# A six-layer decoder on one core: last norms moved into the neighbouring stages, and router logits by column groups

## The chip, the cores and the metric

The kernel runs on 1 core of one Trainium2 chip. The metric is the device time of one execution in microseconds (us), as the median of several runs. The engines are TensorE (PE in the profile; PEld is its weight load), VectorE (DVE), ScalarE (ACT), GpSimd (POOL) and SyncE (SP), which here only issues DMAs.

## The reference, cut to what matters

x is 16 x 128 x 256 (2048 rows of 256 channels). The last two of six sublayers and their norms are the ones that the change touches:

```python
    x = _layernorm(x + _L1_attn_ref(...), axis=-1)
    x = _layernorm(x + _L1_xattn_ref(x, ctx_2048, ...), axis=-1)   # n4 in the kernel before
    x = _layernorm(x + _L1_ffn_ref(x, w_gate, w1, w3, w2), axis=-1)  # n5 in the kernel before
    return x

    def _L1_ffn_ref(hidden_states, w_gate, w1, w3, w2):
        x = hidden_states.reshape(-1, H)                 # 2048 x 256
        logits = x @ w_gate                              # 256 x 8
        logits = SOFTCAP * jnp.tanh(logits / SOFTCAP)
        probs = jax.nn.softmax(logits, axis=-1)
        _, idx = jax.lax.top_k(probs, TOPK)              # 2 of 8 experts
        weights = probs * jax.nn.one_hot(idx, E).sum(-2)
        for e in range(E):
            h = jax.nn.silu(x @ w1[e]) * (x @ w3[e])
            out = out + h @ w2[e] * weights[:, e:e + 1]
```

_layernorm subtracts a row's mean and divides by the root of its variance plus 1e-5, with no gain and no offset.

## The kernel before, in words

The rows are held in SBUF as X[p, b, c]: 16 batches b of 128 rows, a row per partition p. The program is a chain of layers. Each is a block with one instruction stream per engine, written out by hand in program order, and semaphores between the streams. Between two layers `layer` frees the semaphores and all engines meet at a barrier (L139). The layers at the end are `quant_layer` (its main part is `attention`), `norm_layer` "n4", `moe_layer` and `norm_layer` "n5".

`attention` has 128 units: 8 head groups w by 16 batches b, u.n = 16 w + b. `in_steps` writes out, on each engine, steps 0, 1, 2, ...; in step s a stage with lag k works on unit s - k. On PE the stages of a step are queries(0), keys_values(0), turn_p(3), turn_q(1), output(5), turn_k(1), values(3), scores(1). queries writes the bank bQ (L1387, L1388) and may begin once DVE's apply_q (L1607) has read the unit before. output (L1464) needs z from POOL (L1582); DVE's residual (L1651) adds its result to X. In the last head group, w = 7, the row's value is final with the residual, and DVE takes its statistics (row_stats, L1655). After unit 127 has entered there are five more steps, in which fewer and fewer stages have work: the drain.

n4 (L203 and on) first works out from row_stats the means and deviations of 8 batches at a time on DVE (L371 to L376), takes the power -0.5 on POOL (L351), and scales the rows on DVE (L385, six of eight batches) and ACT (L328, two). SP loads the router's weights moe_gate and the first four pieces (1 MB each) of the experts' weights w1 and w3 (L1685, into w_low), and stores the normed rows to two DRAM tensors, sums and rows_x (L1697). PE runs three products that only keep it busy (L288), transposes X (L301), and multiplies it with the gate: 32 products with 128 rows of XT as the stationary operand and 8 moving columns (L280). Its groups of four batches wait for copies from PSUM by ACT (L322) and DVE (L395). The weights w1, w3 are split into high (rounded, fp32r) and low (what is left) halves, piece by piece: ACT makes high (`split_high`, L1703), DVE low (`split_low`, L1708), and for the four pieces in BY_PE PE makes low (`subtract`, L1810 and L1811) and ACT copies it back (`keep`, L1900).

`moe_layer` first works out the routing: DVE's chain L1969 to L2046 (softmax, top two, a place for each row in tiles of 128 rows of one expert), with counts and a map made on PE (L1818, L1825). Then POOL gathers the rows of a tile from rows_x (L1950), PE transposes them (L1850), multiplies by w1 and w3 (`up`, L1863 to L1865), transposes (L1873) and multiplies by w2 (`down`, L1884), and POOL adds the result to sums in DRAM (L1960), one add after the other (semaphore d_add). There are 39 tiles. Before the first tile PE waits for the routing, for all halves of the weights and for w2.

n5 loads sums back in two halves (L244), takes statistics (L366), scales, and stores the output in two halves (L249).

## Time and profile before

| | us |
|---|---|
| median of 3 runs (lowest, highest) | 1529.4 (1528.71, 1534.27) |
| the profiled execution | 1539.61 |
| its span, first to last instruction | 1537.8 |
| mean granted TensorE clock, of 2.4 GHz | 0.943 |
| PE busy in the span | 1375.2 (89%) |
| DVE busy | 1077.0 (70%) |
| ACT busy | 930.2 (60%) |
| POOL busy | 816.5 (53%) |

The page's shares are means over layers that have different limits; what counts here is which wait ends last at the places that are changed. The profiled execution is 10.2 us longer than the median of the timed ones. Of the program's 1537.8 us the attention ends at 1235.5, n4 runs from 1236.6 to 1261, the experts' layer from 1262.0 to about 1510, and n5 from 1514.5 to the end.

### The profile page before, as it was taken

To read this page: it belongs to the slowest core of one execution; us is meant where nothing else is said; L and a number is where in the kernel's file an instruction comes from. 1 tells how busy PE (TensorE), PEld (TensorE's weight loads), DVE (VectorE), ACT (ScalarE), POOL (GpSimd) and SP (SyncE) were. 2 spreads that over 40 slices of the span, in tenths; PEclk is the share of its full clock that TensorE was granted. 3 is DMA by queue.
4 is the path that set the end of the run, shared out by engine and by line. 5 is a ranking of instruction groups with operands and counts; after the bars stand their busy time and mean duration, and the time that the engine had idled before them with its cause. 6 is when DMAs were issued, how large, how long until landed. Compare 5 with 4: busy or idle time off the path is not lost. (4 is left out here: it accounts for less than half of the span.)

```text
span 1537.8 us, 27930 instructions
## 1 busy us (share of the span) xinstructions
PE 1375.2 (89%) x8307; PEld 1112.7 (72%) x8324; DVE 1077.0 (70%) x2565; ACT 930.2 (60%) x3122; POOL 816.5 (53%) x853
## 2 busy tenths in 40 slices
PE   7599467998579999999999999999999978999990
PEld 3343355765248999999988888888888765888880
DVE  1599676887577888888888887778888746333323
ACT  3199315776447878788887777777777735232220
POOL 2377103654206767677796676756765511455441
PEclk9699789999689999999999999999999969999996
DMA  3363001000010100001001010000000067333323
GB/s 124 115 227 132 31 26 42 2 1 1 1 42 1 43 1 29 26 1 46 12 24 51 1 42 1 29 14 1 1 1 1 1 213 245 48 50 52 52 42 117
DMA packets 45811, 72.76 MB, mean 47 GB/s; under 512 B 3772, under 2 KB 32388, under 8 KB 43364
## 3 DMA queue, kind: packets, MB, share of 16 engines
q1 hardware_dynamic: 32804, 44.00, 8.6%
q0 software_dynamic: 7488, 10.23, 4.2%
q10 hardware_dynamic: 5376, 16.78, 2.9%
q8 instruction: 71, 1.16, 0.3%
q14 instruction: 72, 0.59, 0.1%
HBM read 50.94 MB, written 20.05 MB: 46 GB/s over the span
## 5 line engine op out<-in xcount | busy, mean ns | idle before, releaser
L1513 ACT ACTIVATE pr_<-ps,neg_ 128x128 f32<-128x128 f32 x512 | 181.4, 366 | 68.4 <-DVE neg_ L1621 67.6
L1571 POOL TENSOR_TENSOR rstd<-var,half 128x6 f32<-128x6 f32 x128 | 172.2, 1345 | 10.2 <-POOL var L1566 0.4
L1530 ACT ACTIVATE y<-ps,invsm 128x128 bf16<-128x128 f32 x512 | 145.9, 369 | 24.7 <-PE ps L1453 24.5
L1582 POOL TENSOR_TENSOR z<-t,m 128x512 fp32r<-128x512 f32 x128 | 148.6, 1161 | 4.0 <-DVE t L1647 4.0
L1566 POOL TENSOR_TENSOR var<-stat,deps 128x6 f32<-128x6 f32 x128 | 25.5, 199 | 230.8 <-DVE stat L1601 230.8
L1435 PE MATMUL ps<-qkt 128*128 128x128 f32 x1024 | 145.4, 285 | 2.3 <-ACT qkt L1497 1.2
L1435 PEld LDWEIGHTS ps<-qkt 128*128 128x128 f32 x1024 | 124.8, 192 | 29.6 <-issue 26.9
L1464 PE MATMUL ps<-phi,z 128*128 128x256 f32 x512 | 138.9, 303 | 3.6 <-POOL z L1582 3.4
L1575 POOL TENSOR_TENSOR pr_<-pr_,rec_ 128x512 f32<-128x512 f32 x128 | 133.5, 1043 | 4.7 <-DVE rec_ L1628 4.7
L1453 PE MATMUL ps<-XT 128*128 128x256 f32 x512 | 132.1, 381 | 2.2 <-ACT XT L1521 2.2
L1464 PE MATMUL ps<-plo,z 128*128 128x256 f32 x512 | 128.3, 283 | 0.0
L1596 DVE BATCH_NORM_STATS2 stat<-ps 128x6 f32<-128x256 f32 x256 | 97.7, 424 | 33.9 <-PE ps L1388 33.8
L1621 DVE TENSOR_REDUCE neg_<-ps 128x4 f32<-128x512 f32 x128 | 88.5, 691 | 41.9 <-PE ps L1435 41.9
L1960 POOL DMA_INDIRECT sums<-f_ys,f_ids x39 | 61.8, 1583 | 105.0 <-PE ps L1850 83.3
L1387 PE MATMUL ps<-whi,xq 128*128 128x512 f32 x256 | 112.3, 439 | 4.5 <-DVE XT L1607 3.0
L967 ACT ACTIVATE d_pr<-ps,neg 128x128 f32<-128x128 f32 x256 | 89.8, 404 | 37.5 <-DVE neg L1006 37.5
L1497 ACT ACTIVATE qkt<-ps,aff 128x512 f32<-128x512 f32 x128 | 99.2, 775 | 12.7 <-PE ps L1418 12.7
L861 POOL TENSOR_TENSOR d_pr<-d_pr,rec 128x512 f32<-128x512 f32 x64 | 66.6, 1041 | 74.4 <-DVE rec L1015 74.4
L1513 ACT ACTIVATION_READ_ACCUMULATOR pr_<-ps,neg_ 128x1 f32 x512 | 103.9, 203 | 0.0
L1388 PE MATMUL ps<-wlo,xq 128*128 128x512 f32 x256 | 101.9, 398 | 0.0
L1464 PEld LDWEIGHTS ps<-phi,z 128*128 128x128 f32 x512 | 97.4, 190 | 4.9 <-POOL z L1582 4.9
L1521 ACT ACTIVATE XT<-ps 128x512 f32<-128x512 f32 x128 | 76.9, 601 | 38.9 <-PE ps L1444 34.8
(307 smaller groups left out, 3922.3 us busy)
## 6 DMA issues: line engine op xcount, KB each, us to landing
centred<-raw_weights ACTq DMA_DIRECT2D x8, 1024.0 KB, 4.2
w_low<-w_dram SPq DMA_DIRECT2D x8, 1024.0 KB, 11.6
aw_st<-centred SPq DMA_DIRECT2D x7, 1024.0 KB, 4.9
raw_weights<-wself_dram ACTq DMA_DIRECT2D x4, 1024.0 KB, 10.5
raw_weights<-wcross_dram ACTq DMA_DIRECT2D x4, 1024.0 KB, 15.3
w<-w_dram SPq DMA_DIRECT2D x2, 2048.0 KB, 21.1
aw_rows<-wproj_dram SPq DMA_DIRECT2D x7, 512.0 KB, 3.9
xin<-xT_dram SPq DMA_DIRECT2D x4, 512.0 KB, 8.3
```

The source lines that it names most:

```text
L1387: pe.matmul(bQ[:, :], x[:, k, :], whi[:, u.slot, 0, k, :], start=(k == 0), stop=False)
L1388: mm = pe.matmul(bQ[:, :], x[:, k, :], wlo[:, u.slot, 0, k, :], start=False, stop=(k == CB - 1))
L1435: mm = pe.matmul(bS[:, h * S:(h + 1) * S], qkt[:, u.par, h, :], qkt[:, u.par, HEADS + h // 2, :], start=True, stop=True)
L1453: mm = pe.matmul(bO[:, two], kvn[:, u.place, 2 + w, :], pt[:, u.par, two], start=True, stop=True)
L1464: mm = pe.matmul(bW[:, 0:C], z[:, u.par, h * S:(h + 1) * S], part[:, u.slot, h // 2, h % 2, :], start=(h == 0 and part is phi), stop=(h == ...
L1497: act.activation(qkt[:, u.par, 0:HEADS, :], bTQ[:, :].rearrange("p (h s) -> p h s", h=HEADS), ACT.Identity, bias=a[:, 1:2], scale=a[:, 0:1 ...
L1513: ins = act.activation(pr[:, u.par, h, :], bS[:, h * S:(h + 1) * S], ACT.Exp, bias=neg[:, u.par, h:h + 1], accum_out=tot[:, u.par, h:h + 1])
L1530: ins = act.activation(y[:, u.par, h * S:(h + 1) * S], bO[:, h * S:(h + 1) * S], ACT.Copy, scale=invsm[:, head:head + 1])
L1571: pool.tensor_tensor(rstd[:, u.par, 0:6], v, half[:, :], ALU.pow).then_inc(s_rstd, 1)
L1575: pool.tensor_tensor(pr[:, u.par, :, :], pr[:, u.par, :, :], rec[:, u.par, :].unsqueeze(2).to_broadcast([P, HEADS, S]), ALU.mult).then_inc ...
L1582: pool.tensor_tensor(z[:, u.par, :], t[:, u.par, :], m[:, u.par, :], ALU.subtract).then_inc(s_z, 1)
L1596: dve.bn_stats(stat[:, u.par, 6 * h:6 * h + 6], two)
```

## The change

1. **The norm n4 goes into the attention.** For the last head group DVE turns a batch's statistics into mean and variance (row_moments, lag 6), POOL adds the epsilon and takes the power (row_deviation, lag 6), DVE scales the row in place (row_normed, lag 7), and SP stores it to rows_x and sums, a batch at a time (lag 7).
2. **PE gets products that only keep it busy** (keep_warm): 7 ahead of each of the last four outputs, and 10 behind the last. The three of n4 are gone with it.
3. **A gate layer takes n4's place.** PE transposes X without a wait, then forms the logits transposed: the gate's weights, padded from 8 to 32 columns, are the stationary operand, 512 columns of XT the moving one, and the four groups of rows go to four groups of 32 PSUM partitions (two rounds of four products instead of 32 products). DVE copies the 128 x 512 result, PE turns it back with four transposes. ACT splits one piece of weights here (it split two in n4) and DVE none (it split one).
4. **In the experts' layer** ACT splits the pieces 1 and on; BY_PE is (0, 2, 3, 7) instead of (1, 2, 3, 7); DVE's low half of piece 1 stands where that of 4 stood, and that of 4 behind the routing with 5 and 6. The wait for w2 moves from ahead of the first tile to its first use, in down.
5. **n5 goes into the experts' layer**, without a barrier between: four loads, statistics and stores of four batches, mean and variance by DVE's aggregate instruction, deviation and shift on POOL, the scaling on ACT (four batches of each of the first two quarters, two of each of the last two) and DVE (the rest).

```diff
+ROWS = 32
+WARM_UNITS, WARM_PRODUCTS, WARM_AT_END, BY_PE = 4, 7, 10, (0, 2, 3, 7)
...
-            layer(norm_layer, "n4", experts=experts, stats=row_stats)
         if stop > 5:
+            layer(gate_layer, experts)
             layer(moe_layer, experts)
-            layer(norm_layer, "n5", back=False, through=(io["sums"], io["out"]))
...
+                def store_rows(u):
+                    if not u.last:
+                        return
+                    sp.wait_ge(s_normed, u.b + 1)
+                    for name in ("rows_x", "sums"):
+                        sp.dma_start(io[name][u.b * S:(u.b + 1) * S, :], X[:, u.b, :]).then_inc(rows_stored, 16)
+                in_steps([(load_weights, 0), (load_context, 0), (store_rows, 7)])
...
+                def keep_warm(u):
+                    if u.n < UNITS - WARM_UNITS:
+                        return
+                    pe.wait_ge(s_qn, UNITS)
+                    for _ in range(WARM_PRODUCTS):
+                        pe.matmul(bQ[:, :], columns(CROSS, 0)[:, 0, :], whi[:, u.slot, 0, 0, :], start=True, stop=True)
+                in_steps([(queries, 0), (keys_values, 0), (turn_p, 3), (turn_q, 1), (keep_warm, 5), (output, 5), (turn_k, 1), (values, 3),
                           (scores, 1)])
+                for _ in range(WARM_AT_END):
+                    pe.matmul(bQ[:, :], columns(CROSS, 0)[:, 0, :], whi[:, 1, 0, 0, :], start=True, stop=True)
...
+                def row_deviation(u):
+                    pool.wait_ge(s_mean, u.b + 1)
+                    pool.tensor_scalar(spread[:, b], mean_var[:, u.b, 1:2], LN_EPS, None, ALU.add).then_inc(s_spread, 1)
+                    pool.wait_ge(s_spread, u.b + 1)
+                    pool.tensor_tensor(scale[:, b], spread[:, b], half[:, 0:1], ALU.pow).then_inc(s_scale, 1)
...
+                def row_moments(u):
+                    if u.last:
+                        dve.wait_ge(s_row, u.b + 1)
+                        dve.bn_aggr(mean_var[:, u.b, :], row_stats[:, u.b, :]).then_inc(s_mean, 1)
+                def row_normed(u):
+                    if u.last:
+                        dve.wait_ge(s_scale, u.b + 1)
+                        dve.tensor_scalar(X[:, u.b, :], X[:, u.b, :], mean_var[:, u.b, 0:1], scale[:, u.b:u.b + 1],
+                                          ALU.subtract, ALU.mult).then_inc(s_normed, 1)
...
+def gate_layer(experts, nc, io, sem, sbuf, X, XT, small, ident, ps, col, cols):
+    gate, across = experts.gate, experts.w2[:, 0, 0:W512]
+        def _(sp):
+            sp.dma_start(gate[:, :, 0:E], io["w_gate"].rearrange("(k p) n -> p k n", p=P)).then_inc(d_gate, 16)
+            experts.load_up(sp, io, range(0, UP_PIECES // 2))
+        def _(pe):
+            for tg in range(NTG):
+                for k in range(CB):
+                    for j in range(4):
+                        mm = pe.transpose(ps[tg * 2 + k][:, j * P:(j + 1) * P], X[:, tg * 4 + j, k * P:(k + 1) * P], ident[:, :])
+                    mm.then_inc(s_turned, 1)
+            pe.wait_ge(d_gate, 16)
+            for k, s_free in enumerate((s_left, s_right)):
+                for tg in range(NTG):
+                    pe.wait_ge(s_free, tg + 1)
+                    mm = pe.matmul(dots[tg * ROWS:(tg + 1) * ROWS, :], gate[:, k, :], XT[:, k, tg * W512:(tg + 1) * W512],
+                                   start=(k == 0), stop=(k == CB - 1))
+            mm.then_inc(s_dots, 1)
+            pe.wait_ge(s_across, 1)
+            for j in range(4):
+                mm = pe.transpose(bL[:, j * P:(j + 1) * P], across[:, j * P:(j + 1) * P], ident[:, :])
+        def _(act):
+            for tg in range(NTG):
+                act.wait_ge(s_turned, tg * 2 + 1)
+                act.activation(XT[:, 0, tg * W512:(tg + 1) * W512], ps[tg * 2][:, :], ACT.Copy).then_inc(s_left, 1)
+            experts.split_high(act, 0)
+        def _(dve):
+            for tg in range(NTG):
+                dve.wait_ge(s_turned, tg * 2 + 2)
+                dve.tensor_copy(XT[:, 1, tg * W512:(tg + 1) * W512], ps[tg * 2 + 1][:, :]).then_inc(s_right, 1)
+            dve.wait_ge(s_dots, 1)
+            dve.tensor_copy(across, dots[:, :]).then_inc(s_across, 1)
...
+                for q in range(QUARTERS):
+                    sp.dma_start(X[:, quarter(q), :], sums[quarter(q).start * P:quarter(q).stop * P, :].rearrange(
+                        "(b p) c -> p b c", p=P)).then_inc(d_sum[q], 16)
...
-                pe.wait_ge(experts.w2_loaded, experts.W2_LOADS)
                 pe.wait_ge(s_ids, 2)
...
+                    if u.peeled and u.n == 0:
+                        pe.wait_ge(experts.w2_loaded, experts.W2_LOADS)
...
-                experts.split_low(dve, 4)
+                experts.split_low(dve, 1)
...
+                experts.split_low(dve, 4)
                 experts.split_low(dve, 5)
                 experts.split_low(dve, 6)
```

How instructions stand, each line one group in program order: line, instruction, what it writes and reads, size, count. PE at the end of the attention (whi, xq: the keeping-busy products; phi, plo, z: the output), in the layer behind it (moe_gate: the logits) and at the start of the experts' layer (w_low), before:

```order
L1464 MATMUL ps<-phi,z 128x256
L1464 MATMUL ps<-plo,z 128x256
L1358 UNCONDITIONAL_BRANCH
L266 UNCONDITIONAL_BRANCH
L288 MATMUL ps<-ident 128x512 x3
L301 MATMUL ps<-ident,X 128x128 x16
L280 MATMUL ps<-moe_gate,XT 128x8 x8
L301 MATMUL ps<-ident,X 128x128 x8
L280 MATMUL ps<-moe_gate,XT 128x8 x8
L301 MATMUL ps<-ident,X 128x128 x8
L280 MATMUL ps<-moe_gate,XT 128x8 x16
L238 UNCONDITIONAL_BRANCH
```

and in the changed kernel:

```order
L1434 MATMUL ps<-phi,z 128x256
L1434 MATMUL ps<-plo,z 128x256
L1447 MATMUL ps<-whi,xq 128x512 x10
L1321 UNCONDITIONAL_BRANCH
L1726 UNCONDITIONAL_BRANCH
L1731 MATMUL ps<-ident,X 128x128 x32
L1738 MATMUL ps<-XT,moe_gate 32x512 x8
L1743 MATMUL ps<-ident,w 128x128 x4
L1716 UNCONDITIONAL_BRANCH
L1873 UNCONDITIONAL_BRANCH
```

The transposes now run in one piece ahead of the logits, and 8 wide products stand for 32 narrow ones.

DVE in the last two steps of the attention that had work for it (y, m, t: the rounding of a unit; X: the residual), before:

```order
L1632 TENSOR_SCALAR y<-y 128x512
L1638 TENSOR_SCALAR m<-y 128x512
L1643 TENSOR_SCALAR m<-m 128x512
L1647 TENSOR_TENSOR t<-y,m 128x512
L1651 SCALAR_TENSOR_TENSOR X<-ps,pscale,X 128x256
L1655 BN_STATS row_stats<-X 128x6
L1651 SCALAR_TENSOR_TENSOR X<-ps,pscale,X 128x256
L1655 BN_STATS row_stats<-X 128x6
L1358 UNCONDITIONAL_BRANCH
```

and in the changed kernel:

```order
L1635 TENSOR_TENSOR t<-y,m 128x512
L1639 SCALAR_TENSOR_TENSOR X<-ps,pscale,X 128x256
L1643 BN_STATS row_stats<-X 128x6
L1653 TENSOR_SCALAR X<-X,row_mean_var,row_scale 128x256
L1648 BN_AGGR row_mean_var<-row_stats 128x2
L1639 SCALAR_TENSOR_TENSOR X<-ps,pscale,X 128x256
L1643 BN_STATS row_stats<-X 128x6
L1653 TENSOR_SCALAR X<-X,row_mean_var,row_scale 128x256
L1648 BN_AGGR row_mean_var<-row_stats 128x2
L1653 TENSOR_SCALAR X<-X,row_mean_var,row_scale 128x256 x2
L1321 UNCONDITIONAL_BRANCH
```

Each step of the last head group has one aggregate and one scaling more on DVE; the scaling stands behind the statistics of a younger batch and ahead of the next apply_q.

DVE at the end of the program (f_ys: a tile's result), before:

```order
L2070 TENSOR_SCALAR f_ys<-ps,f_weight 128x256 x2
L1793 UNCONDITIONAL_BRANCH
L355 UNCONDITIONAL_BRANCH
L366 BN_STATS n_st<-X 128x6 x8
L371 TENSOR_TENSOR n_m<-n_st 128x8
L372 TENSOR_TENSOR n_m<-n_st 128x8
L373 TENSOR_TENSOR n_m<-n_st 128x8
```

and in the changed kernel:

```order
L2161 TENSOR_SCALAR f_ys<-ps,f_weight 128x256 x2
L2168 BN_STATS f_stats<-X 128x6 x4
L2171 BN_AGGR f_mean_var<-f_stats 128x2 x4
L2168 BN_STATS f_stats<-X 128x6 x4
L2171 BN_AGGR f_mean_var<-f_stats 128x2 x4
L2168 BN_STATS f_stats<-X 128x6 x4
L2171 BN_AGGR f_mean_var<-f_stats 128x2 x4
L2168 BN_STATS f_stats<-X 128x6 x4
L2171 BN_AGGR f_mean_var<-f_stats 128x2 x4
L2177 TENSOR_SCALAR X<-X,f_mean_var,f_rstd 128x256 x4
```

There is no branch into another block between the last tile and the statistics, and four batches are taken at a time.

## Rows read from the trace of the kernel before

**Rows 1.** Windows: length, busy us of PE, PEld, DVE, ACT, POOL; clock, DMA share, GB/s.

```profile
1220.80:1234.60 13.80, 8.84 (x51) 7.00 (x49) 7.87 (x21) 5.07 (x20) 5.08 (x5) 0.88 0.00 1
...
1262.00:1295.40 33.40, 27.70 (x116) 17.39 (x116) 28.64 (x68) 20.94 (x25) 6.89 (x16) 0.95 0.98 326
1295.40:1509.00 213.60, 204.37 (x1014) 172.36 (x1014) 62.25 (x117) 58.94 (x118) 96.32 (x74) 0.98 0.30 47
```

**Rows 2.** Timeline, one step of the attention's last head group: start, length, engine, line.

```profile
1207.74 0.48 DVE L1651 SCALAR_TENSOR_TENSOR X<-ps,pscale,X 128x256 f32<-128x256 f32 x1
...
1208.61 0.67 DVE L1607 TENSOR_TENSOR XT<-ps,rstd 128x512 f32<-128x512 f32 x1
...
1209.51 0.48 PE L1387 MATMUL ps<-whi,xq 128*128 128x512 f32 x1
...
1210.06 0.39 PE L1387 MATMUL ps<-whi,xq 128*128 128x512 f32 x1
1210.30 0.40 PE L1388 MATMUL ps<-wlo,xq 128*128 128x512 f32 x1
...
1213.97 0.48 DVE L1651 SCALAR_TENSOR_TENSOR X<-ps,pscale,X 128x256 f32<-128x256 f32 x1
```

**Rows 3.** Groups by line and shape, POOL's powers: count | busy us, mean ns.

```profile
L1571 POOL TENSOR_TENSOR rstd<-var,half 128x6 f32<-128x6 f32 x128 | 172.2, 1345 | 10.2 <-POOL var L1566 0.4
...
L351 POOL TENSOR_TENSOR n_m<-n_m 128x8 f32<-128x8 f32 x12 | 20.0, 1676 | 33.4 <-DVE n_m L376 33.4
```

**Rows 4.** Timeline, the last output on PE and the last residual on DVE.

```profile
1232.48 0.58 PE L1464 MATMUL ps<-phi,z 128*128 128x256 f32 x1 [2.05 <-POOL z L1582]
...
1234.59 0.48 DVE L1651 SCALAR_TENSOR_TENSOR X<-ps,pscale,X 128x256 f32<-128x256 f32 x1 [2.54 <-PE ps L1464]
```

**Rows 5.** Timeline, n4 with its loads; the last row is of the causal attention.

```profile
1236.66 5.22 PE L288 MATMUL ps<-ident 128*128 128x512 f32 x6 [2.11 <-PEq L139]
...
1237.03 2.35 SPq L1685 DMA_DIRECT2D w_low<-w_dram  x4
...
1241.72 1.91 PE L301 MATMUL ps<-ident,X 128*128 128x128 f32 x16
...
1242.60 1.92 ACT L1703 ACTIVATE w_high<-w_low 128x2048 fp32r<-128x2048 f32 x1 [1.88 <-DMA w_low<-w_dram]
1243.84 1.29 DVE L395 COPY XT<-ps 128x512 f32<-128x512 f32 x2
...
1252.39 1.95 PE L301 MATMUL ps<-ident,X 128*128 128x128 f32 x8
...
324.95 1.07 PE L935 MATMUL ps<-pt_,d_v 128*32 128x256 f32 x16
```

**Rows 6.** Timeline, start of the experts' layer up to its first tile.

```profile
1262.00 0.31 ACT L1891 ACTIVATE f_minus<-ident 128x128 fp32r<-128x128 f32 x1 [6.08 <-PEq L139]
...
1288.62 4.48 DVE L1708 TENSOR_TENSOR w_low<-w_low,w_high 128x2048 fp32r<-128x2048 f32 x2
...
1295.45 0.41 PE L1850 MATMUL ps<-ident,X 128*128 128x128 f32 x2 [3.92 <-DMA w<-w_dram]
```

**Rows 7.** Timeline, the last adds of the experts' layer, and n5.

```profile
1501.02 1.55 POOL L1960 DMA_INDIRECT sums<-f_ys,f_ids  x1 [3.36 <-DVE f_ys L2070]
...
1505.63 1.55 POOL L1960 DMA_INDIRECT sums<-f_ys,f_ids  x1 [3.06 <-DMA sums<-f_ys,f_ids]
1514.50 0.99 SPq L244 DMA_DIRECT2D X<-sums  x2
...
1519.96 2.71 DVE L366 BATCH_NORM_STATS2 n_st<-X 128x6 f32<-128x256 f32 x8 [16.54 <-DMA X<-sums]
...
1527.35 2.03 DVE L385 TENSOR_SCALAR X<-X,n_m 128x256 f32<-128x256 f32 x6
...
1529.41 2.52 SPq L249 DMA_DIRECT2D out_dram<-X  x2
1529.49 1.09 ACT L328 ACTIVATE X<-X,n_m 128x256 f32<-128x256 f32 x2 [1.05 <-DVE n_m L381]
```

180 lines of the change are left out of this document (105 added, 75 removed).

## The prediction

> **What bounds the kernel now.** I read the windows first [rows 1]. The tile loop of the experts' layer (1295.4 to 1509) has PE busy for 204.4 of 213.6 us at a clock of 0.98; the change leaves its code as it is, and likewise the first 118 of the attention's 128 units. What can move are the seams. In the drain of the attention PE is busy for 8.84 of 13.8 us, and before the first tile for 27.7 of 33.4 us. Then I read the seams in the timeline. The last output waits 2.05 us for POOL [rows 4]. n4 takes 25.3 us, from 1236.7 [rows 5] to 1262.0 [rows 6], and much of that is PE at the half clock: 8 transposes take 1.95 us at its end where 16 took 1.91 us before [rows 5]. The first tile waits for w2 [rows 6]. At the end nothing overlaps anything [rows 7]: add, barrier, load, statistics, power, scaling, store.
>
> **Sum, part by part** (times are those of the profiled execution).
>
> *A. The last head group.* The scaling of a row block costs 2.03/6 = 0.34 us [rows 7] and stands ahead of apply_q. apply_q ends at 1208.61 + 0.67 = 1209.28 and PE begins the next queries at 1209.51 [rows 2], so 0.23 us of the 0.34 is hidden by PE's own work. What is queued behind it is apply_q, for that PE's queries wait. The rest with its handing over, which I take as 0.15 us, counts for the 9 steps that still have queries behind a scaling: +1.3 us. Bounds: 0, if PE has more slack than it shows, and 6.1 us, if the scaling and an aggregate (no row; between nothing and one statistics instruction, 2.71/8 = 0.34 us [rows 7]) both come on the path of these 9 steps. POOL's part is hidden: a step is 6.23 us long (residual to residual [rows 2]), and POOL is busy for 53% of the span (the table).
>
> *B. The drain.* 4 x 7 products at 0.24 us each (1210.06 to 1210.30 [rows 2]) are 6.7 us of new PE work. PE is idle for 13.80 - 8.84 = 5.0 us there [rows 1], and the last output, 2.1 us from 1232.48 to the residual at 1234.59 [rows 4], is at the half clock; at the full one it takes about 1.05 us. 6.7 - 5.0 - 1.05 = +0.7 us. Bounds 0 and +3 us. The 10 products behind it (2.4 us) lie beside the chain of C.
>
> *C. From the last statistics to the block's end.* New are, one behind the other: the aggregate 0.2; on POOL an addition, 0.2, and the power of one column. The powers of 6 and 8 columns take 1.345 and 1.676 us [rows 3], 0.166 a column, so about 0.52. The scaling 0.34, the handing over 0.2, and SP's two issues, 0.99 us for two [rows 7]. Together +2.5 us (2.0 to 3.8, if the power of one costs as much as that of six). The gate layer thus begins at 1236.7 + 1.3 + 0.7 + 2.5 = 1241.2.
>
> *D. The gate layer in place of n4.* At the full clock: 32 transposes at 1.91/16 = 0.12 us are 3.8 us. One product with 512 columns took 5.22/3 = 1.74 us at the half clock [rows 5], so 0.87 at the full one. Do four column groups run side by side? The last row of rows 5 is such a case: 8 products of 256 columns into groups of 32 partitions (16 passes) end within 1.07 us, where one after the other they need 8 x 0.435 = 3.5 us. So I take a round of four at 0.95 us. The first round begins at 3.8 and covers the last copy by DVE (1.29/2 = 0.65 us), the second ends at 5.8, the copy of the result (0.8 with its wait) at 6.6, four transposes at 7.3. ACT needs longer: the gate's issue 0.4, the first piece of weights 1242.60 - 1237.03 = 5.6, its split 1.9 us: 7.9. With 1.0 us for the change of blocks 8.9, and 1.0 for a clock that may be low for part of it, since PE idles some 2 us at the barrier: 9.9 (8.9 to 14.5). The experts' layer then begins at 1251.1, against 1262.0: **-10.9 us**.
>
> *E. Before the first tile.* The wait for w2 ended the idle time before [rows 6], so removing it looks like a gain. But DVE's last low half ended at 1288.62 + 4.48 = 1293.10, and a third one, 2.24 us, now stands behind the routing: 1295.34 on the old clock, when w2 had ended at 1295.45. One wait takes the place of the other: **0**. ACT's additional split (1.9 us) is hidden by its own idle time (20.9 busy of 33.4 us [rows 1]), +1.9 if not. The loads are 12.6 MB from 1241.6 on; at 326 GB/s [rows 1] they end at 1280.2, before the first tile at 1251.1 + 33.45 = 1284.5. If PE is warm at the first tile, up to -2.6. All DMA of the row stores lies in the attention, where nothing else loads.
>
> *F. The end.* The add before last was issued at 1501.02 and let the next go at 1505.63, so the last landed at about 1505.63 + 4.6 = 1510.2. n5's load began at 1514.50 [rows 7]; now it begins at 1510.3. The first half (1 MB) took 5.46 us to DVE's first instruction; a quarter is 1.6 us shorter at 326 GB/s: 1514.2. A quarter's statistics are 1.36 us and four aggregates some 0.6, so 8.0 us for all: 1522.2. POOL for the last quarter: three small operations of 0.2 and a power of 4 columns, 1.345 - 0.33 = 1.01: 1.7, 1523.9. ACT's two scalings, 1.09: 1525.0. The second half's store took from 1531.5 to the end at 1537.8, 6.3 us, behind the first; a quarter behind an idle queue I take as 4.4: 1529.4. **-8.4 us** (-4 if an aggregate costs 0.34 and part of the seam stays, -10 if loads and statistics overlap fully).
>
> Sum: -10.9 + 0 - 8.4 = -19.3. Against the profiled execution's own 1539.6 us this is 1520.3, 0.9875 of it; of the median, 1529.4, that makes **1510.2 us**.
>
> **The rivals.**
>
> *1. The gate layer stays at the half clock.* Then 32 transposes take 7.8, two rounds 3.8, copy and turning back 1.9: 13.5 + 1.0 us in place of 9.9, +4.6, 1515 us. For it: PE idles about 2 us ahead of the layer, and 2.05 us of idle time stood ahead of the last output, which ran at the half clock [rows 4]. Against it: 16 transposes ran at 0.12 us each right behind three wide products [rows 5]. The Trainium skill ("TensorE: Matmul & The Clock Gate", Part 4) says that the full clock does not engage for transposes, as they don't count as PE being busy in the same way; by that rule, if PE comes in slow, it stays slow for all of them, and the time is this rival's. The trace neither shows nor refutes it: its slow transposes stand between narrow products. By this rule the rival has 0.20, else I would give it 0.12.
>
> *2. DVE sets the step in the last head group.* A's upper bound, 6.1 in place of 1.3: 1515 us. For it: only 0.23 us of slack. Against it: the aggregate stands behind apply_q, in front of work with slack.
>
> *3. The column groups run one after the other.* 8 x 0.87 = 7.0 in place of 1.9, in part beside the copies: +3.4, 1513.6. The 1.07 us in rows 5 speak against it.
>
> *4. The gain of D is given back before the first tile*, as loads that started late in relation to the routing hold the splits or w2. Then only F is left, about 1521. Against it stand the 4 us of slack in E.
>
> *5. Slower.* One mechanism: in the last 16 batches DVE's scaling waits for POOL in every step, as the power of one column costs as much as that of six. Aggregate, addition, power and scaling in a row are 0.34 + 0.2 + 1.35 + 0.34 = 2.2 us, 16 times 35.7: 1544 us. It decides from (19.3 + 1.3)/16 = 1.3 us a step on. Against it: aggregate and scaling of one batch are a whole step apart, and POOL is idle for about half of a 6.2 us step.
>
> **How the numbers follow.** Forecast 0.53 (1504 to 1514), rival 1 0.20, rival 2 0.11, rival 3 0.06, rival 4 0.07, rival 5 0.02, the rest 0.01. The predicted time is the forecast's, 1510 us. Downwards the bounds are A at 0, D without the 1.0, E at -2.6 and F at -10: 6.5 us, 1503.7. Upwards rivals 1 to 3, alone or with a small second miss, reach 1517.5. Beyond lie 4 and 5. A measurement of this kernel can tell about 0.5% (7.6 us) from no change. All but rivals 4 and 5 are faster by more than that; of rival 4 I count two thirds as within it: faster 0.92, within 0.5% 0.06, slower 0.02.
>
> **What would show it right or wrong.** In the changed kernel's timeline: the attention's step in the last head group stays within 0.2 us of before (A); the last output begins near 1234 and at the full clock (B); the gate layer begins near 1241 and the experts' layer near 1251 (C, D); the two rounds of logits take under 2.5 us (rival 3: 7); the first tile's transposes begin 33.4 us behind the layer's start, released by a split's low half and not by w2 (E); the first load of sums is issued under 0.3 us behind the last add's landing, and the span ends about 19 us behind that (F). The prediction falls if the seams keep their length in another place, above all the 33 us before the first tile, which I take as unchanged.

## The result, and the profile of the changed kernel

The changed kernel takes 1512.28 us (median of 4 runs, 1511.27 to 1513.87), the kernel before 1531.8 us beside it (4 runs, 1528.71 to 1534.27). The ratio is 0.9882, 95% interval 0.9869 to 0.9895, so 16 to 20 us less. The forecast was 1510.0 us in a range of 1503.5 to 1517.5. In a later series on another chip the changed kernel took 1514.35 us against 1531.81, ratio 0.9880 (0.9859 to 0.9900).

The two profiled executions differ by more, 1537.8 against 1510.5 us of span. A part of it comes from ahead of the change. The groups of VectorE's row statistics give a mark that both kernels have; after "x16" stand the shortest, median and longest in ns, then the start of the first and the last. Before, changed kernel:

```profile
L1655 DVE BATCH_NORM_STATS2 row_stats<-X x16: 426/428/428, 1152.3 to 1235.1; 128x6 f32<-128x256 f32 x16
```

```profile
L1643 DVE BATCH_NORM_STATS2 row_stats<-X x16: 426/427/429, 1143.7 to 1230.1; 128x6 f32<-128x256 f32 x16
```

The first row statistic comes 8.6 us earlier in the changed kernel, although nothing ahead of it was changed. Over all 14 profiled executions of this study this mark lies between 1143.7 and 1152.3 us, without relation to the kernel. Whoever subtracts the two spans puts 8.6 us too much down to the change. So I read everything from this mark on, in five stretches. The cuts are the last row statistic, the first transposes of the tile loop, the first and the last weight load of the down products, and the end of the span:

| kernel | statistics | to the loop | to first down | to last down | to the end | sum |
|---|---|---|---|---|---|---|
| before | 82.8 | 60.3 | 11.8 | 195.1 | 35.5 | 385.5 |
| changed | 86.4 | 48.2 | 10.0 | 194.0 | 28.2 | 366.8 |
| changed, again | 86.5 | 48.3 | 10.3 | 193.9 | 28.3 | 367.3 |

18.7 us less, which is what the times show. The last head group lost 3.6 us (3.6 to 4.5 against all three traces of the old attention, whose stretches are 82.8, 81.9 and 82.2 us; in the first of them the last output ran at the half clock), the way to the tile loop gained 12.1, the start and the run of the loop 2.9, the end 7.3.

**The last head group.** The timeline of VectorE and GpSimd in one step, where [rows 2] stood before:

```profile
1208.32 0.48 DVE L1639 SCALAR_TENSOR_TENSOR X<-ps,pscale,X 128x256 f32<-128x256 f32 x1 [0.15 <-PE ps L1434]
1208.60 1.03 POOL L1554 TENSOR_TENSOR pr_<-pr_,rec_ 128x512 f32<-128x512 f32 x1
1208.84 0.43 DVE L1643 BATCH_NORM_STATS2 row_stats<-X 128x6 f32<-128x256 f32 x1
1209.18 0.60 DVE L1653 TENSOR_SCALAR X<-X,row_mean_var,row_scale 128x256 f32<-128x256 f32 x1
...
1209.71 0.68 DVE L1595 TENSOR_TENSOR XT<-ps,rstd 128x512 f32<-128x512 f32 x1
1209.95 0.57 POOL L1570 TENSOR_TENSOR row_scale<-row_spread,half 128x1 f32<-128x1 f32 x1
```

apply_q (L1595) begins 1.39 us behind the residual's start; before, it was 0.87 [rows 2]. Between them stands the scaling (L1653), and it takes 0.60 us, not the 0.34 of n5 [rows 7]. It ends at 1209.78, just behind GpSimd's product (L1554), which ran from 1208.60 to 1209.63. In the same trace 11 of the 16 scalings take 0.60 to 0.62 us, and each of them ends 0.15 us behind the end of a 128x512 operation of GpSimd. The five that met no such operation, or only its last 0.12 us, take 0.38 to 0.41, this one for instance, with GpSimd at rest until 1231.01:

```profile
1230.43 0.40 DVE L1653 TENSOR_SCALAR X<-X,row_mean_var,row_scale 128x256 f32<-128x256 f32 x1
```

**The seam.** The windows (columns as in [rows 1]) and the timeline of the gate stage:

```profile
1229.60:1234.90 5.30, 2.27 (x10) 1.51 (x9) 1.99 (x6) 0.00 (x0) 0.87 (x3) 0.99 0.53 177
1234.90:1237.00 2.10, 2.08 (x10) 2.10 (x11) 0.10 (x1) 0.60 (x1) 0.12 (x1) 0.50 0.13 21
1237.00:1238.30 1.30, 1.30 (x9) 1.30 (x8) 0.59 (x1) 0.55 (x1) 0.00 (x0) 0.55 0.92 343
1238.30:1240.20 1.90, 1.90 (x21) 1.73 (x22) 1.38 (x2) 1.06 (x3) 0.00 (x0) 1.00 1.02 350
1240.20:1244.80 4.60, 2.79 (x20) 1.01 (x20) 1.38 (x2) 2.13 (x3) 0.03 (x1) 1.00 1.02 376
1244.80:1278.30 33.50, 27.75 (x116) 17.45 (x116) 30.85 (x69) 22.67 (x26) 7.04 (x16) 0.95 0.88 302
```

```profile
1231.98 0.41 DVE L1653 TENSOR_SCALAR X<-X,row_mean_var,row_scale 128x256 f32<-128x256 f32 x1 [0.77 <-POOL row_scale L1570]
1233.18 0.45 SPq L1343 DMA_DIRECT2D sums<-X  x1
1234.92 5.26 PE L1731 MATMUL ps<-ident,X 128*128 128x128 f32 x32 [3.06 <-PEq L140]
1240.11 2.23 PE L1738 MATMUL ps<-XT,moe_gate 128*32 128x512 f32 x16
1242.38 0.69 DVE L1760 COPY w<-ps 128x512 f32<-128x512 f32 x1 [1.46 <-PE ps L1738]
1243.12 0.66 PE L1743 MATMUL ps<-ident,w 128*128 128x128 f32 x4 [0.79 <-DVE w L1760]
1244.77 0.15 POOL L2012 IOTA f_token_i<- 128x16 int32 x1 [9.75 <-POOLq L140]
```

The gate stage lasts from 1234.88 (SyncE's issue of the gate's weights) to 1244.77, 9.9 us, where n4 had 25.3. The transposes come in at the half clock (0.50) and the clock rises at about 1238.2, with only transposes behind it. The 16 passes of the logits take 2.23 us. The 33.5 us behind it are as long as before [rows 1], but VectorE is busy for 30.85 of them and not 28.64.

**The start of the loop.** What the first tile waits for is now VectorE and no longer w2 [rows 6]:

```profile
1271.57 6.68 DVE L1702 TENSOR_TENSOR w_low<-w_low,w_high 128x2048 fp32r<-128x2048 f32 x3
1278.35 0.41 PE L1920 MATMUL ps<-ident,X 128*128 128x128 f32 x2 [3.02 <-DVE w_low L1702]
```

**The end.** Timeline, and from the line of the block (L1855) the drain of GpSimd's queue, where the three figures are ns. [rows 7] answer to them:

```profile
1485.52 1.55 POOL L2040 DMA_INDIRECT sums<-f_ys,f_ids  x1 [2.98 <-DMA sums<-f_ys,f_ids]
1489.13 2.02 SPq L1863 DMA_DIRECT2D X<-sums  x4
1493.06 1.41 DVE L2168 BATCH_NORM_STATS2 f_stats<-X 128x6 f32<-128x256 f32 x4 [9.68 <-DMA X<-sums]
1494.97 0.25 POOL L2047 TENSOR_SCALAR f_fall<-f_mean_var 128x4 f32<-128x4 f32 x1 [7.78 <-DVE f_mean_var L2171]
...
1501.75 1.04 POOL L2050 TENSOR_TENSOR f_rstd<-f_spread,f_power 128x4 f32<-128x4 f32 x1
1503.10 1.09 ACT L2006 ACTIVATE X<-X,f_shift,f_rstd 128x256 f32<-128x256 f32 x2 [0.94 <-POOL f_shift L2052]
```

```profile
L1855 POOLq DRAIN  x1: 6690/6690/6690, 1502.8 to 1502.8; - x1
...
L1855 SPq COMPARE_BRANCH  x1: 38/38/38, 1507.2 to 1507.2; - x1
```

From the last add's issue to the end are 25.0 us, before 32.2. SyncE has seen its last store land at 1507.2. The program ends 2.2 us later than that would allow, because GpSimd's drain lasts from 1502.8 to 1509.5. The same drain was there before, 8.21 us long from 1505.4, while the last add was still being issued. Of the 8.9 us between that add (1505.63) and n5's load (1514.50) [rows 7] the add's way to memory took 3.7 (SyncE was past its wait at 1509.4), the rest of the drain 4.2 (to 1513.6) and the barrier 0.9.

### The profile page after: what moved, and what is told of

The parts are those of the page before. It is cut to its first block and busy times, and to the rows that moved or that the text cites. A ratio compares the mean times of both kernels' runs of the same rounds, so it can differ in the third digit from the quotient of the medians.

```text
span 1510.5 us, 27950 instructions
## 1 busy us (share of the span) xinstructions
PE 1362.4 (90%) x8295; PEld 1102.5 (73%) x8312; DVE 1077.2 (71%) x2566; ACT 930.8 (62%) x3126; POOL 830.3 (55%) x897
## 5 line engine op out<-in xcount | busy, mean ns | idle before, releaser
L1550 POOL TENSOR_TENSOR rstd<-var,half 128x6 f32<-128x6 f32 x128 | 172.2, 1346 | 10.1 <-POOL var L1545 0.2
L1545 POOL TENSOR_TENSOR var<-stat,deps 128x6 f32<-128x6 f32 x128 | 25.3, 197 | 223.1 <-DVE stat L1589 223.1
L1554 POOL TENSOR_TENSOR pr_<-pr_,rec_ 128x512 f32<-128x512 f32 x128 | 133.2, 1041 | 3.4 <-DVE rec_ L1616 3.4
L2040 POOL DMA_INDIRECT sums<-f_ys,f_ids x39 | 61.8, 1583 | 101.1 <-PE ps L1920 81.9
L1500 ACT ACTIVATE XT<-ps 128x512 f32<-128x512 f32 x128 | 76.8, 600 | 38.1 <-PE ps L1414 33.5
L1484 ACT ACTIVATE qkt<-ps,aff 128x256 f32<-128x256 f32 x128 | 72.2, 564 | 43.0 <-PE ps L1396 43.0
## 6 DMA issues: line engine op xcount, KB each, us to landing
w_low<-w_dram SPq DMA_DIRECT2D x8, 1024.0 KB, 10.1
raw_weights<-wself_dram ACTq DMA_DIRECT2D x4, 1024.0 KB, 10.3
```

Source lines behind the costliest of these rows:

```text
L1550: pool.tensor_tensor(rstd[:, u.par, 0:6], v, half[:, :], ALU.pow).then_inc(s_rstd, 1)
L1554: pool.tensor_tensor(pr[:, u.par, :, :], pr[:, u.par, :, :], rec[:, u.par, :].unsqueeze(2).to_broadcast([P, HEADS, S]), ALU.mult).then_inc ...
```

## The experiments

All stretches are from profiled executions, in us, cut as in the table above.

| kernel | statistics | to the loop | to first down | to last down | to the end | sum |
|---|---|---|---|---|---|---|
| norm_late | 83.1 | 47.8 | 10.3 | 193.9 | 28.2 | 363.3 |
| no_warm | 86.5 | 49.0 | 10.4 | 193.9 | 28.3 | 368.1 |
| serial_groups | 86.4 | 51.3 | 11.0 | 194.0 | 28.2 | 370.9 |
| w2_only (on before) | 81.9 | 58.8 | 11.1 | 195.1 | 35.8 | 382.7 |
| w2_back | 86.4 | 48.4 | 10.4 | 193.9 | 28.4 | 367.5 |
| pool_piece | 86.3 | 50.5 | 10.4 | 193.9 | 28.2 | 369.3 |
| tail_only (on before) | 82.2 | 60.6 | 11.3 | 195.2 | 28.3 | 377.6 |
| early_drain | 86.4 | 48.3 | 10.1 | 193.9 | 26.1 | 364.8 |
| tail_pool | 86.3 | 48.4 | 10.4 | 193.9 | 27.2 | 366.2 |
| best | 83.1 | 46.4 | 11.4 | 193.9 | 25.8 | 360.6 |
| best_two_queues | 83.1 | 45.8 | 11.4 | 194.0 | 25.7 | 360.0 |

Among the kernels made from the changed one, a stretch that an edit does not touch repeats within 0.4 us, but for the way to the first down product where the clock came in high (11.0 to 11.4 us and not 10.0 to 10.4). Among the three with the old attention it does so within 0.9; the clock differs there too. The changed kernel's own median moved by 2 us between its two series. So an effect of 1 to 4 us is read from its stretch, and the times are beside it. In seven of the runs the median lies above the range that was expected, by 0.3 to 4.8 us (no_warm, serial_groups, norm_late, tail_only, early_drain, tail_pool, pool_piece). The ranges were counted from the first measurement, 1512.3 us (tail_only's from 1531.8), and the first trace of the changed kernel has the shortest part ahead of the mark of all (1143.7 us, the others 1145.0 to 1152.3).

**The scaling's place (norm_late).**

```diff
-in_steps([(row_moments, 6), (apply_kv, 1), (maxima, 2), (query_statistics, 0), (clamp, 4), (key_statistics, 0), ...
-          (residual, 5), (row_normed, 7), (apply_q, 0)])
+in_steps([(apply_kv, 1), (maxima, 2), (query_statistics, 0), (clamp, 4), (row_moments, 6), (row_normed, 7),
+          (key_statistics, 0), ..., (residual, 5), (apply_q, 0)])
```

> The changed kernel with VectorE's two row operations (aggregate and scaling) moved in its step order to just ahead of the key statistics, where it waited 0.45 us for TensorE in the step, and away from apply_q, ahead of which the scaling stood. My theory: the added 0.38 us a step of the last head group came from the scaling's 0.53 us on the path rstd to apply_q to TensorE, while GpSimd's 128x512 subtraction ran beside it; away from there the step goes back to 6.2 to 6.35 us from 6.58, 8 to 9 steps, so 1.8 to 3.2 us less: 1509.1 to 1510.5. Rival: VectorE is as full as its step anyway (or GpSimd's two new operations of 0.8 us hold up its step), then the place of the work doesn't matter: 1512 to 1513.

Measured: 1511.29 us (1509.78 to 1516.85), ratio 0.9867 (0.9846 to 0.9889). The stretch of the statistics goes from 86.4 back to 83.1, so the place of the work costs 3.3 us, and the work itself 0.3 to 1.2 (against 82.8, 81.9 and 82.2 without it). VectorE's timeline in this kernel, and the two groups of scalings, first the changed kernel's, then this one's:

```profile
1205.38 0.17 DVE L1648 BATCH_NORM_AGGREGATE row_mean_var<-row_stats 128x2 f32<-128x6 f32 x1
1205.47 0.38 DVE L1653 TENSOR_SCALAR X<-X,row_mean_var,row_scale 128x256 f32<-128x256 f32 x1
1205.91 0.43 DVE L1589 BATCH_NORM_STATS2 stat<-ps 128x6 f32<-128x256 f32 x1
```

```profile
L1653 DVE TENSOR_SCALAR X<-X,row_mean_var,row_scale x16: 379/602/621, 1156.5 to 1232.0; 128x256 f32<-128x256 f32 x16
```

```profile
L1653 DVE TENSOR_SCALAR X<-X,row_mean_var,row_scale x16: 375/381/415, 1155.7 to 1230.9; 128x256 f32<-128x256 f32 x16
```

The same instruction takes 0.38 us where GpSimd is at rest and 0.60 where its product runs. The theory held; the gain is just above the 1.8 to 3.2 us that it gave. The order also spreads the last stores: the stretch behind the last statistic loses another 0.4 us.

**The filler products (no_warm).**

```diff
-WARM_UNITS, WARM_PRODUCTS, WARM_AT_END, BY_PE = 4, 7, 10, (0, 2, 3, 7)
+WARM_UNITS, WARM_PRODUCTS, WARM_AT_END, BY_PE = 4, 0, 0, (0, 2, 3, 7)
```

> The changed kernel without its 38 filler products in the attention's drain (7 each behind four outputs, 10 at the end). My theory: the fillers cost the drain 0.6 us and the clock of the gate stage rises on the stage's own transposes, so the last residual comes 0.6 us earlier or, at half clock, up to 0.9 us later (the last output's 8 products were at 1.94 us in the kernel before, 1.1 here), and the gate stage stays between 9.9 and 11 us: 1511.5 to 1514 us against 1512.3. Rival: it is the fillers' activity that lets the clock rise at 1238.2; without them the whole gate stage runs at half clock, its logits passes take 4.5 us in place of 2.2 and its 32 transposes 7 in place of 5.3, 14.5 us in all: about 1517 us.

Measured: 1516.59 us (1513.55 to 1522.12), ratio 0.9892 (0.9873 to 0.9912). The statistics' stretch is the same (86.5), so the fillers cost the drain nothing, and the last head group's loss is the scaling's alone. Without them the transposes of the gate stage take 0.7 us more, and the clock rises all the same:

```profile
1243.50:1249.40 5.90, 5.78 (x32) 5.77 (x32) 2.02 (x3) 2.00 (x4) 0.14 (x1) 0.59 0.72 212
1249.40:1254.00 4.60, 3.01 (x22) 1.09 (x20) 1.44 (x3) 2.30 (x2) 0.00 (x0) 1.00 1.03 358
...
1243.62 5.98 PE L1731 MATMUL ps<-ident,X 128*128 128x128 f32 x32 [5.40 <-PEq L140]
1249.52 2.23 PE L1738 MATMUL ps<-XT,moe_gate 128*32 128x512 f32 x16
```

These are windows, then timeline. TensorE had been idle for 5.40 us and then did nothing but 32 transposes. The rival, half clock for the whole stage, falls. Up to the first down product the fillers are worth 0.6 to 1.2 us (59.4 against 58.2 to 58.8 in the traces with them).

**The column groups (serial_groups).** All logits in group 0, a bank for each token group:

```diff
-mm = pe.matmul(dots[tg * ROWS:(tg + 1) * ROWS, :], gate[:, k, :], ...
+mm = pe.matmul(ps[tg * 2][0:ROWS, :], gate[:, k, :], ...
-dve.tensor_copy(across, dots[:, :])
+dve.tensor_copy(across[tg * ROWS:(tg + 1) * ROWS, :], ps[tg * 2][0:ROWS, :])    # for each tg
```

> The changed kernel with the gate's logits all in column group 0, each token group in a bank of its own, and four narrow copies to SBUF where one was. My theory: four products in four column groups run beside one another (16 passes in 2.2 us in the trace of the changed kernel), in one group they follow one another: 16 passes of 512 columns at 0.44 us are 7.0 us, of which at most 1 us hides beside the copies of the transposed rows; gate stage 13.9 to 14.7 us instead of 9.9, 1516.3 to 1517.1 us. Rival: the column groups are served one after another anyway or the stage is bound by the copies out of PSUM: no change, 1512.3.

Measured: 1519.6 us (1519.03 to 1520.67), ratio 0.9916 (0.9900 to 0.9933). TensorE's timeline:

```profile
1239.01 3.68 PE L1731 MATMUL ps<-ident,X 128*128 128x128 f32 x32 [3.06 <-PEq L140]
1242.62 7.05 PE L1738 MATMUL ps<-XT,moe_gate 128*32 128x512 f32 x16
```

16 passes take 7.05 us one after the other and 2.23 side by side: a factor of 3.2. The stretches to the first down product are 3.5 to 4.1 us longer, 62.3 against 58.2 to 58.8. The transposes here ran at the full clock from the start, though nothing ahead of them differs from the changed kernel: 3.68 us against 5.26. Whether the stage comes in at the full or the half clock varies between executions of the same code.

**The wait for w2, alone and taken back (w2_only, w2_back).** The same edit on the kernel before, and undone in the changed one:

```diff
 pe.wait_ge(s_left, len(BY_PE) * PIECE * CB)
-pe.wait_ge(experts.w2_loaded, experts.W2_LOADS)
...
 pe.wait_ge(s_he, u.n + 1)
+if u.peeled and u.n == 0:
+    pe.wait_ge(experts.w2_loaded, experts.W2_LOADS)
```

> The kernel before with one line moved: TensorE's wait for w2 from ahead of the tile loop to ahead of the first product that reads it. My theory: in the kernel before that wait ended last, 2.2 us behind VectorE's last low half; now VectorE releases the loop and the first down product comes later than the loads' landing: 2.0 to 2.3 us less, 1529.7 us. Rival: w2 lands later than the first product wants it, or the first tiles wait for something else, and the gain is given back: 1532.

> The changed kernel with TensorE's wait for w2 put back ahead of the tile loop. The loads of the experts' block landed by about 1271 us in the trace of the changed kernel (the DMA share falls from 1.10 to 0.54 there), 7 us ahead of VectorE's last low half at 1278.25. My theory: the other parts have already brought the loads forward so far that the moved wait is worth nothing any more: from the gate stage's start to the loop's first transposes 43.4 us as before, within 0.5. Rival, the prediction's own figure of 1280.2 us for the end of the loads: the wait ends last again and costs 2 us, 45.4.

Measured: w2_only 1530.34 us (1526.4 to 1536.78), ratio 0.9986 (0.9967 to 1.0005), which the times cannot tell from nothing. In the trace the loop's transposes come 1.5 us earlier and not 2.2, for another wait takes the place:

```profile
1280.27 4.48 DVE L1708 TENSOR_TENSOR w_low<-w_low,w_high 128x2048 fp32r<-128x2048 f32 x2
...
1286.32 0.66 PE L1849 MATMUL ps<-ident,X 128*128 128x128 f32 x2 [3.15 <-DMA X<-rows_x,f_ids]
```

VectorE is done at 1284.75, and TensorE waits until 1286.32 for the first gather of rows, which GpSimd issued at 1280.13 while w2 was still coming in. w2 landed at 1286.8, so the moved wait itself saved some 0.9 us here; the rest of the 1.5 us is w2, which landed 59.3 us behind the last statistic and not 60.0 as before. The rival was half right: another wait gives part of the gain back. w2_back took 1514.36 us in one run; its way to the loop is 48.4 us against 48.2 and 48.3, and the wait still ends with VectorE. In the changed kernel w2 landed at 1272.65, 5.7 us ahead of the first tile, and the traffic falls:

```profile
1268.00:1270.00 2.00, 2.00 (x18) 1.86 (x16) 2.00 (x1) 2.00 (x2) 0.00 (x0) 1.00 1.10 347
1270.00:1272.00 2.00, 1.35 (x5) 0.77 (x5) 1.93 (x7) 0.65 (x1) 0.56 (x1) 1.00 0.54 172
1272.00:1274.00 2.00, 2.00 (x7) 1.00 (x6) 2.00 (x2) 1.19 (x2) 1.70 (x2) 1.00 0.24 68
```

So the moved wait is worth about 0.9 us by itself, in one trace, and nothing in this change; the other parts brought the loads forward.

**Relieving VectorE ahead of the loop (pool_piece).**

```diff
 (GpSimd)
+experts.split_low(pool, 1)
 pool.wait_ge(s_ids, 2)
 (VectorE)
-experts.split_low(dve, 1)
+experts.split_low(dve, 4)
...
-experts.split_low(dve, 4)
 experts.split_low(dve, 5)
```

> The changed kernel with the low half of piece 1 made by GpSimd, idle from 1247 to 1270 there, and VectorE's three others moved up one place. My theory: VectorE's last low half holds up TensorE's tile loop by 3.0 us; without one of four 2.28 us subtractions it ends at 1276.0 instead of 1278.3, where TensorE's and ScalarE's own last piece ends as well: 2.2 us less, unless GpSimd's subtraction (about 5 us at 1.27 us for 512 columns) stretches VectorE's small operations beside it by up to 1 us: 1510.1 to 1511.1. Rival: the loads of w2 (to 1280.2) or the slowed chain on VectorE take the place of the wait, and nothing is left: 1512.3.

Measured: 1515.93 us (1513.58 to 1521.96), ratio 0.9901 (0.9874 to 0.9929). The way to the loop is 2.2 us longer instead of 2.2 shorter, outside forecast and rival. GpSimd's row, then VectorE's:

```profile
1251.29 4.53 POOL L1702 TENSOR_TENSOR w_low<-w_low,w_high 128x2048 fp32r<-128x2048 f32 x1 [2.78 <-ACT w_high L1697]
```

```profile
1251.35 0.28 DVE L2078 TENSOR_REDUCE f_pm<-XT 128x16 f32<-128x128 f32 x1
1251.67 4.30 DVE L2079 TENSOR_TENSOR XT<-XT,f_pm 128x128 f32<-128x128 f32 x1
1256.01 0.29 DVE L2082 SCALAR_TENSOR_TENSOR XT<-XT 128x128 f32<-128x128 f32 x1
```

VectorE's comparison, 0.29 us elsewhere, took 4.30 us: it stood until GpSimd's subtraction was over. The reduction before it, with one input, went through at its usual 0.28 us. I had expected a stretching by up to 1 us in all. The Trainium skill ("SBUF — State Buffer", section "SBUF: two separate sides") says that VectorE and GpSimd share a pair of ports as an exclusive lock, which a VectorE operation with two inputs in SBUF or in a fast mode needs, and that the loser fully blocks. The trace agrees: 4.30 us instead of 0.29. The same lock fits the scaling's 0.60 us. There it is inferred: the comparison here and the 11 long scalings of the changed kernel all end 0.15 us behind the end of GpSimd's operation (1255.97 behind 1255.82, 1209.78 behind 1209.63), and the scaling's length falls back to 0.38 where GpSimd rests.

**The last part alone (tail_only).** The kernel before with the last norm inside the experts' block, by quarters; n5 is gone, and all else is as before.

> The kernel before with part 5 alone: the last norm inside the experts' block, by quarters, in place of a norm stage of its own. My theory: the end shortens by 7.3 us as in the trace of the changed kernel, for it hangs on nothing ahead: 1531.8 - 7.3 = 1524.5 us, 1523.5 to 1525.5. Rival: part of the 7.3 us came with the other parts (less DMA work late, or GpSimd's drain shortened by the earlier stores), then 1526 to 1529.

Measured: 1525.81 us (1523.3 to 1529.22), ratio 0.9960 (0.9943 to 0.9976), 6.2 us less in the median. The end is 28.3 us long, as in the changed kernel (28.2), against 35.5. The median, 0.3 us above the range, would not decide between theory and rival; the stretch does: the last part stands by itself. The drain is here as well, and has the same length:

```profile
L1802 POOLq DRAIN  x1: 6692/6692/6692, 1516.0 to 1516.0; - x1
```

**GpSimd's drain (early_drain).**

```diff
 skewed(pool, NT // PER, PER, [(gather, 0), (add, ADD)], PEEL)
+pool.drain()
 pool.memset(power[:, :], -0.5).then_inc(s_fall, 1)
```

> The changed kernel with a drain of GpSimd placed right behind the last add, ahead of the memset of the powers, where GpSimd is idle for 7.8 us. In the changed kernel and in the one with the last part alone GpSimd's own drain at the end of the last block takes 6.69 us from 1502.8 (1516.0) and ends the program. My theory: GpSimd pays it once after its indirect transfers, wherever it first drains; placed at 1487 it hides in the wait for the statistics, the drain at the end is short, and the program ends with SyncE, released at 1507.4 instead of 1509.5: 1.5 to 2.2 us less, 1510.1 to 1510.8. Rival: the 6.7 us belong to the drain at a block's end whatever came before: two drains, the same end, 1512.3, or later by what the first one holds up the first power (up to 1 us, 1513.3).

Measured: 1515.04 us (1512.36 to 1518.2), ratio 0.9893 (0.9869 to 0.9917). The median doesn't show the gain; in the profiled execution (1513.0 us) the part ahead of the mark alone was 2.6 us longer than in the changed kernel's. The end's stretch does show it: 26.1 us against 28.2. The two drains of GpSimd in this kernel:

```profile
L2044 POOLq DRAIN  x1: 8213/8213/8213, 1488.0 to 1488.0; - x1
```

```profile
L1855 POOLq DRAIN  x1: 307/307/307, 1505.7 to 1505.7; - x1
```

The long one now lies beside the load and the first statistics; GpSimd begins the first quarter right when VectorE hands it over (1497.80). The one at the block's end takes 0.31 us. So the price is paid once behind the indirect transfers, at the first drain, wherever that stands. The theory held. The price is also the same in every kernel: a drain's row begins while GpSimd's instruction before it still runs, and counted from that instruction's end the drain lasts 6.4 to 6.5 us in all 14 traces (before: 1507.18 to 1513.62, changed kernel: 1503.06 to 1509.52, here: 1489.73 to 1496.17). In the changed kernel the last add had landed at 1489.05, so the drain at the block's end did not wait for it.

**GpSimd's share of the last norm (tail_pool).** Of the four instructions a quarter GpSimd keeps the addition and the power:

```diff
-pool.tensor_scalar(fall[:, quarter(q)], mean_var[:, quarter(q), 0], -1.0, None, ALU.mult)
-pool.tensor_tensor(shift[:, quarter(q)], fall[:, quarter(q)], rstd[:, quarter(q)], ALU.mult)
+dve.scalar_tensor_tensor(shift[:, quarter(q)], mean_var[:, quarter(q), 0], -1.0, rstd[:, quarter(q)], ALU.mult, ALU.mult)
```

> The changed kernel with GpSimd's work of the last norm cut from four instructions to two for each quarter (spread and power; negation and shift are one instruction on VectorE). My theory: GpSimd's 2.03 us for each quarter is the bound of the stretch from the first statistics to the last store, VectorE's are 1.70; at 1.4 us of GpSimd a quarter VectorE becomes the bound, the last scaling ends about 1.0 us earlier and GpSimd's own drain of 6.7 us starts about 1.0 us earlier: 1511.3 us (1510.9 to 1511.7). Rival: the stores' way to memory or a fixed end sets it: 1512.3.

Measured: 1513.33 us (1512.05 to 1517.64), ratio 0.9877 (0.9853 to 0.9902); the end's stretch is 27.2 us against 28.2, as expected. But only GpSimd's drain, which ends the program, moves: counted from the last down product's weight load SyncE is released after 24.8 us, in the changed kernel after 24.9. The last scaling ends 0.8 us earlier, but the stores take as long as before, 8.0 and 8.1 us from the first one's issue to the last one's landing. For SyncE's release the rival was right.

**All together (best, best_two_queues, after_again).** best is norm_late, early_drain and tail_pool in one. best_two_queues adds:

```diff
+def store_sums(u):            # ScalarE, behind its other stages
+    if u.last and u.b >= B - 3:
+        act.wait_ge(s_normed, u.b + 1)
+        act.dma_start(io["sums"][u.b * S:(u.b + 1) * S, :], X[:, u.b, :]).then_inc(rows_stored, 16)
```

> The changed kernel with three edits of the earlier runs together: VectorE's row operations ahead of the key statistics, GpSimd's drain right behind the last add, and the last norm's small work shared between GpSimd and VectorE. In the traces the stretch from the first row statistics to the end was 366.8 us in the changed kernel and 3.5, 2.0 and 0.6 us less with one edit each; the last 3.1 us from the last down product to the end are independent of the first edit, and with the drain gone SyncE's release is the end, which the shared work brings forward by another 1.0. My theory: the gains add up, 360.2 us for that stretch (359.5 to 361.5), and 6 us less than the changed kernel in the time. Rival: the drain and the shared work cut the same wait, and one of the two is worth nothing: 361.5 to 363 us.

> The changed kernel as it is, beside the others on the same chip. It tells how far the stretch ahead of the first row statistics, which no part of the change touches, moves the time from one execution to the next: that stretch took 1143.7 to 1152.3 us in the profiled executions so far. My theory: the time is 1512 to 1516 us, the stretch from the first row statistics to the end 366.8 us within 1 us, so the spread of the time is all from ahead of it. Rival: the changed stages themselves vary, by their clock, and the stretch comes out 2 us or more from 366.8.

> The combined kernel with ScalarE issuing the stores of sums for the last three batches, so that SyncE has one store a batch there and not two. My theory: behind VectorE's last scaling SyncE's two issues (0.43 to 0.48 us each) are on the chain from the last residual to the gate stage, 4.7 us in the kernel with the operations moved; one less is 0.4 us less. Rival: the barrier's own steps or ScalarE's issue take its place, no difference of 0.2 us or more.

Measured, side by side on one chip: the changed kernel 1514.35 us (1512.31 to 1514.96), best 1508.06 us (1506.84 to 1511.1), best_two_queues 1507.39 us (1507.03 to 1513.23), the kernel before 1531.81. Ratios to before: 0.9880 (0.9859 to 0.9900), 0.9844 (0.9825 to 0.9863), 0.9849 (0.9826 to 0.9871). So best takes 6.3 us off the changed kernel, 6.2 to 6.7 by the stretches. after_again gives 367.3 for the sum of its stretches, 366.8 the first time: of the 2.6 us between the two spans 2.1 come from ahead of the mark. That is the greater part, as I expected, and not all.

The end of best is 25.8 us, not 25.1: drain and shared work don't add up. GpSimd's last drain is over at 1503.1, and SyncE's wait for the last store alone sets the end. The shared work hardly moves that wait, as tail_pool showed, and is worth 0.3 us here (26.1 to 25.8):

```profile
L1855 POOLq DRAIN  x1: 1162/1162/1162, 1502.0 to 1502.0; - x1
...
L1855 SPq COMPARE_BRANCH  x1: 38/38/38, 1508.1 to 1508.1; - x1
```

The whole, 360.6 us, lies in the forecast's range (359.5 to 361.5), since the other stretches came out lower; for the end the rival has the mechanism: one of the two edits is worth almost nothing beside the other. The second queue brings the gate stage to 4.3 us behind the last residual (1228.1 to 1232.4), from 4.7; between the two kernels' times there is no difference that could be told.

## Why the prediction was right, and where it was off

The forecast of 1510.2 us missed the median by 2 us, and its case is the one that came: the gain is made in the seams, the tile loop keeps its length within 1.1 us. As a ratio it was 0.9875, and 0.9882 was measured. So close a hit is in part luck, for misses of several terms cancel. The terms, each counted from the mark:

- **A and B, +2.0 forecast, +3.6 measured.** Here the mechanism was right and the size was off, above all of the term of 0.34 us for the scaling. I took it from n5 [rows 7], where GpSimd was at rest; beside GpSimd's product it takes 0.60, and apply_q begins 0.52 us later. Less the 0.23 us of slack that is 0.37 us a step, and the step did grow from 6.23 to 6.59 us, beyond the 0.2 that I had allowed. norm_late takes 3.3 us back. The working looked at whether GpSimd had time for its own new part (it has) and not at what GpSimd does to VectorE beside it. B's 0.7 us isn't there: no_warm takes nothing off the statistics' stretch.
- **C, +2.5 forecast, +3.2 measured.** From the last statistic to TensorE's first work in the next stage it was 1.6 us (1235.1 to 1236.66) and is 4.8 (1230.09 to 1234.92). The pieces that I counted have about their size: power 0.57, scaling 0.41, an issue of SyncE 0.45. Missing were two short waits: the scaling of the batch before stands ahead of the last aggregate (0.2 us), and SyncE was still issuing the stores of the batch before when the last scaling ended (0.3). The rest is in the power's and the barrier's steps.
- **D, 9.9 us forecast and measured.** The parts differ: transposes 5.26 for 3.8, as the clock was low for 3.3 us, and the logits 2.23 for 1.9. I had put 1.0 aside for the clock. That split is borne out as well: in best, whose stage ran at the full clock, it lasted 8.8 us with ScalarE's split ending last, as in the sum (8.9); at the low clock TensorE's own chain ends last. Together with A to C the experts' layer begins 101.1 us behind the mark, before 109.7: -8.6 for -10.9.
- **E, 0 forecast.** For the way from the experts' stage's start to its first tile that is right: 33.58 us against 33.45, with VectorE's third low half in w2's place. The figure behind it holds too, if both are counted from the mark: w2 landed 129.0 us behind it (1272.65), forecast were 127.9 (1280.2 on the clock of the trace before, whose mark stands 8.6 us later). In the texts ahead of pool_piece and w2_back I set 1280.2 against the new trace without that shift, and so read it as some 8 us later than it is. w2_back shows the moved wait worth nothing, as that figure implies. From the first transposes to the first down product it is 1.8 us less, as the clock is back at 1.00 sooner (its mean over the first 7 us of the loop is 0.76 for 0.55); the bound of -2.6 held that. The 1.1 us of the tile loop (0.03 us a tile, in every kernel with the gate stage) I did not foresee, and no run here shows its cause.
- **F, -8.4 forecast, -7.3 measured.** The load begins 3.6 us behind the last add's issue (4.7 forecast), and the statistics 3.9 us later, as worked out. I took the gap between the add's landing and n5's load for the change of stages and so as gone. Most of it was GpSimd's drain, which only moves to the program's end and holds it for 2.2 us: that is the term that I had at nothing. early_drain gets 2.1 of them back.

The sum is -18.7 us for -19.3: A, C and F cost 3.4 us more than forecast, E gave 2.8 more.

The rivals: 1 (half clock throughout) falls, since the clock rose within the transposes in every execution that came in low. The rule of the Trainium skill ("TensorE: Matmul & The Clock Gate", Part 4) that the full clock doesn't engage for transposes is not borne out: with nothing but fp32 transposes from 1234.92 on the granted clock went from 0.50 to 1.00 at 1238.2, and in no_warm likewise behind 5.40 us of idle time. The rival's price of 4.6 us may have been too high as well; no execution stayed low throughout, so that isn't shown. But a full clock in the stage is given back: best went through the gate stage at 1.00 and reached the loop 1.2 us sooner, but then needed 11.4 us to the first down product, not 10.0. Its windows of the gate stage's transposes and of the loop's first 4.9 us:

```profile
1235.90:1239.30 3.40, 3.36 (x31) 3.39 (x32) 1.90 (x3) 1.88 (x4) 0.14 (x1) 1.00 0.38 98
...
1278.10:1283.00 4.90, 3.78 (x11) 3.01 (x12) 0.85 (x2) 2.16 (x4) 2.65 (x3) 0.57 0.28 80
```

The clock is 1.00 in the first and 0.57 in the second. Of the eight executions with the gate stage, the fillers and the splits unchanged, the six that came in low took 53.4 to 54.0 us from the stage's first transpose to the first down product, the two that came in high 53.4 and 53.6. Rival 2 (6.1 us in A) came in part: VectorE's scaling does set the step, for 3.3 us, while the 0.37 us a step leave nothing for the aggregate. Rival 3 is refuted by the 2.23 us and priced by serial_groups at 3.5 to 4.1 us. Rivals 4 and 5 did not come: no gain was given back before the first tile, and VectorE waits for GpSimd's scale only for the very last batch, 0.77 us.
